# Output stores of a first convolution block, issued by GpSimd or by SyncE

## The reference, cut to what matters

```python
def _denoise_block(x, w1, b1, w2, b2, w3, b3, a, b, c):
    trip = _triplets(x)                    # each channel with its two neighbours
    xf = trip.reshape(B * T, C, H, W)
    o = a * _conv_reflect(xf, w1, b1, 1, 2) + b * _conv_reflect(xf, w2, b2, 2, 4) \
        + c * _conv_reflect(xf, w3, b3, 4, 8)          # 5x5, dilations 1, 2 and 4
    return jnp.tanh(o).reshape(B, T, H, W)
y = _denoise_block(x, ...)                 # first block
z = _denoise_block(y, ...)                 # second block
x = x + z                                  # x enters the blocks as _gn(x)
```

## Time and profile before

| | us |
|---|---|
| median of three runs | 5207.72 |
| lowest and highest run | 5193.19, 5213.15 |
| the profiled execution, its own time | 5195.99 |
| its span in the trace | 5194.2 |
| TensorE busy in the span | 4878.0 (94%) |
| VectorE, ScalarE, GpSimd busy | 3721.9, 3385.3, 1775.1 |

### The profile page before, as it was taken

The page is one execution under the profiler, slowest core; times in us unless marked ns, Lnnn a source line. Parts: engine busy times, 40 slices in busy tenths (PEclk is TensorE's granted clock), DMA queues, the critical chain, the costliest instruction groups (busy, mean ns, idle before and its releaser), DMA issues. The chain is left out here.

```text
span 5194.2 us, 176617 instructions
## 1 busy us (share of the span) xinstructions
PE 4878.0 (94%) x76605; PEld 2891.1 (56%) x76605; DVE 3721.9 (72%) x6707; ACT 3385.3 (65%) x3511; POOL 1775.1 (34%) x2217
## 2 busy tenths in 40 slices
PE   4999999999999999999999979997777899999998
PEld 2454444444455578555766744344555566666665
DVE  4743453453534888888888868887999688888888
ACT  1322222222223888888888878785998789989997
POOL 1223223223224222222222100003776355555556
PEclk9999999999999999999999989999999999999999
DMA  9888888789777778887887769996887455655654
GB/s 265 244 239 263 229 245 253 215 248 272 215 207 209 221 221 232 238 224 223 237 232 238 222 211 322 326 321 244 309 308 263 116 153 149 153 151 151 153 150 119
DMA packets 399631, 1167.57 MB, mean 225 GB/s; under 512 B 120617, under 2 KB 121256, under 8 KB 329002
## 3 DMA queue, kind: packets, MB, share of 16 engines
q1 hardware_dynamic: 313752, 1075.55, 69.5%
q0 software_dynamic: 82944, 78.34, 5.5%
q10 hardware_dynamic: 2162, 2.39, 0.2%
HBM read 683.58 MB, written 453.51 MB: 219 GB/s over the span
## 5 line engine op out<-in xcount | busy, mean ns | idle before, releaser
L726 PE MATMUL c_p<-c_w,wc 128*32 128x512 f16 x27648 | 1522.4, 380 | 45.7 <-issue 37.5
L804 ACT ACTIVATE c_t<-c_p,cbias,cscale 128x512 f32<-128x512 f32 x512 | 398.1, 777 | 1311.0 <-PE c_p L726 1310.9
L726 PEld LDWEIGHTS c_p<-c_w,wc 128*32 128x32 f16 x27648 | 766.0, 96 | 773.5 <-issue 62.7
L726 PE MATMUL c_p<-c_w,w 128*32 128x512 f16 x19456 | 1131.4, 379 | 5.4 <-issue 5.4
L726 PEld LDWEIGHTS c_p<-c_w,w 128*32 128x32 f16 x19456 | 712.8, 96 | 355.3 <-issue 11.8
L631 DVE TENSOR_SCALAR c_y<-c_t 128x512 f16<-128x512 f32 x256 | 111.2, 434 | 666.2 <-ACT c_t L804 664.7
L1800 PE MATMUL f_P<-f_qh,f_wt 64*64 64x512 f16 x4608 | 545.7, 378 | 1.8 <-DVE f_t L1696 1.8
L1800 PE MATMUL f_P<-f_hl,f_wt 64*64 64x512 f16 x4608 | 545.3, 379 | 0.0
L810 ACT ACTIVATE c<-c_w 64x2052 f16<-64x2052 f16 x256 | 492.9, 1925 | 6.3
L809 ACT ACTIVATE c<-c_w 64x2052 f16<-64x2052 f16 x256 | 492.5, 1924 | 6.3
L1961 POOL TENSOR_TENSOR f_y<-f_y,f_x 128x512 f32<-128x512 f32 x256 | 330.8, 1292 | 448.9 <-DVE f_hl L1675 442.8
(11 more groups left out here) (275 smaller groups left out, 7984.4 us busy)
## 6 DMA issues: line engine op xcount, KB each, us to landing
c_w<-xs SPq DMA_DIRECT2D x576, 264.0 KB, 8.4
d_x<-x SPq DMA_DIRECT2D x128, 1024.0 KB, 7.6
x<-d_x SPq DMA_DIRECT2D x128, 1024.0 KB, 5.1
ys<-c_y POOLq DMA_DIRECT2D x576, 132.0 KB, 9.3
c_w<-ys SPq DMA_DIRECT2D x144, 528.0 KB
xs<-a_hl SPq DMA_DIRECT2D x70, 1056.0 KB, 12.5
a_x<-in_x SPq DMA_DIRECT2D x256, 256.0 KB, 7.5
a_x<-in_x SPq DMA_DIRECT2D x128, 512.0 KB, 4.9
```

Source lines behind the costliest of these rows:

```text
L726: t = p.matmul(pg[32 * j:32 * j + 32, :], weights[:, var], source[:, j, at:at + NW], start=start, stop=stop, tile_position=(0, 32 * j))
L804: s.activation(tt_[n % 3][:, :], pp[:, n % 4, :], ACT.Tanh, bias=cbias[:, blk:blk + 1], scale=cscale[:, blk:blk + 1]).then_inc(c_act, 1)
```

## The change: who issues the stores of the first block

Of the 64 units of the first block, 14 are called crowded: units 0 to 3, and those with u % 16 in (15, 0, 1). GpSimd goes on issuing the stores of these, with semaphores `c_yp` of their own. SyncE issues the stores of the other 50 units, on the semaphores `c_yd`, right after it has issued the window loads of the same group. Whoever waited for the stores of earlier units now waits for both kinds.

```diff
-        def n_ys(u):
-
-            return 16 * sum(8 + 4 * (place(r)[2] in (0, 7)) for r in range(u % 2, u, 2))
+        def crowded(u):
+
+            return u < NU and (u < 4 or u % 16 in (15, 0, 1))
+
+        def stored(e, u):
+
+            for busy, done in ((False, c_yd), (True, c_yp)):
+                n = 16 * sum(8 + 4 * (place(r)[2] in (0, 7)) for r in range(u % 2, u, 2) if crowded(r) == busy)
+                if n:
+                    e.wait_ge(done[u % 2], n)
...
                     if u >= 2 and g == 0:
-                        v.wait_ge(c_yd[u % 2], n_ys(u))
+                        stored(v, u)
...
-                def store_y(u, g):
+                def store_busy(u, g):
                     blk, b, p, half = place(u)
                     q.wait_ge(c_pad, 8 * u + 2 * g + 2)
...
-                        q.dma_start(dram(ys, ...), y[m::2]).then_inc(c_yd[u % 2], 16)
+                        q.dma_start(dram(ys, ...), y[m::2]).then_inc(c_yp[u % 2], 16)
...
-                            store_y(u, g)
+                            if crowded(u):
+                                store_busy(u, g)
...
-                        e.wait_ge(c_yd[0], n_ys(r))
-                        e.wait_ge(c_yd[1], n_ys(r + 1))
+                        stored(e, r)
+                        stored(e, r + 1)
...
+                def store_y(u, g):
+                    blk, b, p, half = place(u)
+                    e.wait_ge(c_pad, 8 * u + 2 * g + 2)
+                    y = yt[u % 2][:, g].rearrange("p l w -> p (l w)")
+                    for m, gp, slot in [(0, p, 1), (1, p + 1, 0)] + [(1, 0, 0)] * (p == 0) + [(0, 8, 1)] * (p == 7):
+                        e.dma_start(dram(ys, ...), y[m::2]).then_inc(c_yd[u % 2], 16)
...
                         if blk:
                             store_x1(u, g)
+                        elif not crowded(u):
+                            store_y(u, g)
```

More of the change, by code:

```diff
@@ L346, in layer0 @@
         c_yd = [sem(f"c_yd{i}") for i in range(2)]
+        c_yp = [sem(f"c_yp{i}") for i in range(2)]
         c_xd = [sem(f"c_xd{i}") for i in range(2)]
@@ L873, in store_y @@
                     for m, gp, slot in [(0, p, 1), (1, p + 1, 0)] + [(1, 0, 0)] * (p == 0) + [(0, 8, 1)] * (p == 7):
-                        q.dma_start(dram(ys, pair(b, gp, slot, 16 * half) + g * 4 * RW, [[RW, 4], [VP, 16], [1, RW]]), y[m::2]).then_inc(c_yd[u % 2], 16)
+                        q.dma_start(dram(ys, pair(b, gp, slot, 16 * half) + g * 4 * RW, [[RW, 4], [VP, 16], [1, RW]]), y[m::2]).then_inc(c_yp[u % 2], 16)
                 def near_weights(i):
@@ L958, in load_res @@
                         e.dma_start(xwin(u)[m::2], rows(x, u, m, NW, NH * NW)).then_inc(c_xd[u % 2], 16)
+                def store_y(u, g):
[3 more added lines that the diff above has]
+                    for m, gp, slot in [(0, p, 1), (1, p + 1, 0)] + [(1, 0, 0)] * (p == 0) + [(0, 8, 1)] * (p == 7):
+                        e.dma_start(dram(ys, pair(b, gp, slot, 16 * half) + g * 4 * RW, [[RW, 4], [VP, 16], [1, RW]]), y[m::2]).then_inc(c_yd[u % 2], 16)
                 def store_x1(u, g):
```

## The result

Five runs of the changed kernel gave a median of 5170.7 us (5166.33 to 5175.35), against 5209.69 us for the kernel before beside it. The ratio is 0.9929, with a 95% interval of 0.9911 to 0.9948: 37 us faster, give or take 10. Run once more later, beside other runs of the kernel before, it gave 5166.49 us and 0.9929 (0.9911 to 0.9946). Its profiled execution has a span of 5164.4 us, 29.8 less than the 5194.2 of before.

The account below looks back on a forecast made before the run. TensorE was taken to bound the kernel, losing 35.2 us to late instruction fetches. Only the fetch term counted, -20 us with all others 0, taking the median 5207.7 to 5188 us; range 5158 to 5215.

Parts of the forecast that it names:

- the case that was held likeliest: Whole kernel: gain of 10 to 32 us, 5176 to 5198 us, chance 0.42.
- all of it goes: Rival: every instruction fetch in time, 35 us of waits and some 5 us that follow go, 5168 us; chance 0.17.
- The fetch: TensorE's instruction fetch in the first block: two thirds of 29.3 us of exposed waits go, 20 us gained.
- What bounds and what is lost: First block: TensorE bounds, losing 75 us of 1460, of which 35.2 us are issue waits from late instruction fetches.
- The discount for the bursts of 1056 KB: Fetch gain in the first block: taken below the second block's rate (23 us), as that block has no such bursts.
- The loads behind the stores: SyncE's window loads: delayed by stores, TensorE might wait at units 14, 30 and 46 only; 0 to 39 us, taken 0.
- The buffer c_y: VectorE's wait in group 0 for stores of unit u - 2: met by 4 us, at worst missed by 9; worth 0.
- SyncE, 0: SyncE in the first block: 416 issues at the median are 248 us and fit in its 568 us of waits; 0.
- The rival in which it becomes the bound: SyncE late for good above a mean of 1.37 us per issue; 5264 us, slower; chance 0.13.
- DMA time: The 16 DMA engines in the first block: the move saves about 13 us, nobody waits for it; counted 0.
- Nothing changes: Rival: the fetch waits behind all data on the DMA engines, whichever queue, and the gaps only move; 5208 us, chance 0.28.
- The signs: Window 180 to 1640 us: q0 near 5%, issue wait near 15 us, no c_w wait, SyncE's TensorE wait down 200 us.

Follow-up runs that it names:

- The control: Changed kernel with all 576 first-block stores back on GpSimd, on the new semaphores: 5212.1 us, 1.0016 to the kernel before.
- the half version: Changed kernel with GpSimd also issuing the stores of units with u % 4 in (2, 3), about half of the 416: 5178.3 us, 0.9955 to the kernel before.
- the version without the rule for image changes: Changed kernel with only units 0 to 3 on GpSimd, SyncE issuing all other first-block stores: 5214.3 us, 1.0027 to the kernel before.
- The throttled GpSimd version: All 576 stores on GpSimd, each group's issued only when those of the group before have landed: 5733.5 us, 1.1015 to the kernel before.
- small stores beside: Changed kernel plus one extra 4 KB GpSimd DMA to scratch for each store of the 50 units: 5178.4 us, 0.9955 to the kernel before.

## Why the prediction was right, and where it was off

The time of 5170.7 us lies in the range of 5158 to 5215, on the side that was forecast, but outside the case that was held likeliest (5176 to 5198), and nearer to *all of it goes* (5168). Two terms of the sum were off in opposite directions, the fetch by 20 us and the window rows by 13.5; that they partly cancelled is luck, and the range was wide enough for either case.

- *What bounds and what is lost.* Right. The loss was in TensorE's issue waits, and they are where the gain is. The control and the half version confirm that GpSimd's part in the stores is the cause. The other 40 us, taken as statistics and weights, held 5 us that belonged to these stalls.
- *The fetch, 20 us.* The mechanism was right and the size was off. Two thirds of the exposed 29.3 us were taken to go; 32.3 of 35.2 us went, and with what followed from the stalls 40.5 us, all that the rival *all of it goes* had counted. The discount for the bursts of 1056 KB was the mistake. They still make the fetch late (27 gaps over 10 us, 28 before), but seldom by so much that TensorE runs dry. The 5.1 us of waits in the ten units that keep GpSimd went altogether: the two waits left are in units 29 and 50. So a wait is not fixed to the unit whose stores GpSimd issues.
- *The loads behind the stores, 0 to 39 us, taken at 0.* They cost 8.9 us of waits at two image changes (6.3 us on the second run), and 13.5 us with the lower clock behind them, which no term of the sum had. The place was named rightly, unit 14; the value lay above the one chosen and well inside the bounds.
- *The buffer c_y, 0.* VectorE did wait, 49.1 us in three waits, but TensorE had nothing of it. That the same wait is dear when it falls ahead of the statistics was named in the working (2 us free), and the version without the rule for image changes showed it: three waits of TensorE, 25.1 us.
- *SyncE, 0.* Issue median 0.567 us, forecast about 0.6. Its free time fell by 296 us, for 248 reckoned; at the mean of 0.74 us in place of the median, the 416 issues are 309. The rival in which it becomes the bound needed a mean of 1.37 us and did not come; the version without the rule comes near it locally, at image changes.
- *DMA time, 0 to -13 us, counted as 0.* The queues q1 and q0 together held the engines for 81.3% and now for 76.2%, 74 us less of 1460 while moving a little more. Far more than 13. The price per MB that was taken for SyncE's stores is the mean over all of q1; in the trace such a store is 64 packets of 2112 bytes at 91 ns, 0.36 us of the 16 engines and not 0.46, and the window loads' packets of 8448 bytes fell from 463 to 430 ns as well. It may be why the gain went to its upper end; that is argued and not shown.
- *Nothing changes*, the rival that followed the Trainium skill, "DMA: Bandwidth & Descriptors", section "Issuing engines are not separate DMA queues", was wrong here. The same bytes went over the same 16 engines, and the issuer mattered by 0.7% of the kernel.
- *What is left over.* The median fell by 39 us and the ratio says 37, the profiles fell by 29.8: 24.1 by the end of the first block and 6.0 in the second, 5 of them around 2395 us, where the kernel before has a dip of the clock that comes elsewhere or not at all in other profiles. The other 7 us lie within the interval.
- *The signs.* q0 at 4.1% (near 5 forecast), new stores at 0.567 us (0.6) came about, and nearly so SyncE's wait for TensorE, down by 192 us (200 or more); an issue wait near 15 us (2.9) and no wait on `c_w` (two) did not.

What stays open is why GpSimd's stores hold up the fetch and the same stores on a third hardware queue don't. Three readings are left. One is that GpSimd issues without being held (its issues take 622 ns at the median and at most 2247 before), and so adds to the line on the DMA engines when it is longest, where SyncE and ScalarE are stopped at the issue. The throttled GpSimd version was to test that and disturbed too much else. The second is the 8-byte packets of its large stores. The third is plain DMA time: its stores take more of the engines than those of SyncE or ScalarE, and no version put that time back in another way. The data queues together hold the engines for 81.3% before and 81.7% in the control, for 79.3% in the half version, 76.2% in the changed kernel and 74.5% with ScalarE, and the issue wait goes largely with it. Against it: without the 416 stores they are at 70.4%, and the issue wait is 5.7 us, no less than in the changed kernel; and small stores beside and unit 14 on GpSimd stand at 77.2% and 77.1% with 6.6 and 12.2 us.

## What to carry to other kernels

When an engine that should be busy shows idle time put down to "issue", look at its instruction queue among the DMA queues before anything in the program: here fetches that came late cost 35 us of idle time and 40 us in all, and moving 132 KB stores out of GpSimd's queue took that away without touching TensorE's program. Reckon a stall from one eviction to the next, not by its idle time: two waits of 8.9 us cost 13.5. Before an issuer takes on more DMAs, compare its waits, not its busy time, with what it will issue, and look at where its backlog is longest: three units at each of three image changes decided between a gain of 0.7% and a loss of 0.3%. A wait that a buffer covers for the main work may have uncovered work behind it in the same engine's queue.

## What the runs showed of the hardware

- TensorE's instruction fetch comes as one packet of 16.4 KB every 7 us. When it comes late enough, TensorE stands still: all 22 issue waits of before end 2.2 to 2.9 us after a packet begins that came 7.7 to 16.6 us after the one ahead. The issue waits are 28.8 to 35.2 us in 1460 us with 527 stores of 132 KB from GpSimd, 21.5 with 341 of them, 6.6 with 416 stores of 4 KB beside the changed kernel, and 2.9 to 4.4 and 6.2 with the 416 large ones from SyncE or ScalarE.
- After a stall TensorE's granted clock can stand at 0.50 (1.2 GHz): for 6.8 us behind the 3.64 us of wait at 502 us, for 3.4 us behind 3.93 us at 811 us before. It does not follow each stall: waits of 3.14 to 3.40 us before left it at 1.00.
- Hardware-queue issues hold their engine when the DMA engines are full: the stores took up to 4.17 us each to issue on SyncE and 11.57 us on ScalarE, with medians of 0.57 and 0.53. GpSimd's took 0.62 us at the median and 2.25 at most.
- The move lowered the DMA engines' busy share for slightly more work, from 0.82 to 0.77. In the traces a store of 64 rows of 2112 bytes is, from GpSimd, 32 packets of 4224 bytes (214 ns each), 96 of 8 bytes and 16 of 4 (10 ns each), 0.50 us of the 16 engines; from SyncE, 64 packets of 2112 bytes (91 ns each), 0.36 us. In the version without the 416 stores q1 stands at 66.1% for 276.93 MB:

```profile
q1 hardware_dynamic: 67178, 276.93, 66.1%
```

Against the 72.1% for 330.75 MB of the changed kernel, the stores added 6.0% of 1460 us, 88 us or 0.21 us each; other packets took longer without them (8448 bytes: 457 ns, 430 in the changed kernel). The like figure for GpSimd is the 81.3% of both data queues before less the 70.4% without, 159 us for 403 stores or 0.39 us each. It is this 0.39 that goes with 0.21, and the 0.50 with the 0.36. The kernels do slightly different amounts of work in the window, so both differences are rough.
